# Scatters of a batch as 16 pairs behind named matmul groups, and fills of the last batch as plain DMAs on SP's queue

## The chip, the cores and the metric

The kernel runs on one core of a Trainium2 chip. The metric is the device time of one execution in microseconds (us). The kernel before takes 2137.58 us, the median of three runs (2136.33 to 2138.60).

## The reference

A transformer block over 16 sequences of 512 tokens with 256 features: a layer norm, causal attention with 16 heads of 16 dimensions and rotary positions, a mixture of 32 experts of which each token uses 4, and a shared feed-forward part.

```python
xn = _layernorm(x)
x = x + attention(xn, Wq, Wk, Wv, Wo) + ffn(xn, ...)

# the mixture, for every token n of the 16 * 512
scores = softmax(flat @ router_w.T + router_bias)
topk_scores, topk_idx = top_k(scores, 4)
topk_scores = topk_scores / topk_scores.sum(-1)
h = silu(flat @ gate_w[e].T) * (flat @ up_w[e].T)      # each expert e
out = sum over the 4 chosen e of topk_scores * (h @ down_w[e].T)
out = out + silu(flat @ sgate_w.T) * (flat @ sup_w.T) @ sdown_w.T
```

## The kernel before

There are three phases, with a barrier of all engines between them.

**Phase A** (phase_a) goes over the 16 batches (sequences). For a batch it computes attention, the shared feed-forward part and the routing, and writes each normalised token to four places in DRAM, one for each expert chosen. The tensor values has a region of 8192 rows for each of the 32 experts, and an expert's tokens lie there from the region's start; table has an entry (token number, weight) for each row. **Phase BC** (phase_bc) takes the experts' rows in 288 blocks of 128, applies the expert, and scatters the results into y_dram. **Phase D** (phase_d) sums a token's four results and the rest, and stores them.

A block of phase BC is read whole, so the rows behind an expert's last token, up to the block's end, must hold something harmless. The last batch of phase A therefore also writes 128 rows of zeros behind each expert's last token. This is the step fill.

Phase A is one list of steps, ORDER, which every engine walks through in the same order and in which it takes the steps that it has a handler for. The matrix multiplications of a step run on TensorE (PE), and the same names stand for the copies and exponentials on ScalarE (ACT), the reductions on VectorE (DVE) and the sums on GpSimd (POOL). The list mixes two batches: attention and feed-forward steps of batch b, and projection and routing steps of batch b+1 (NEXT_STEPS). An engine does its steps strictly in turn, so an instruction that waits holds all behind it on that engine. Batch 0 has its own copy of the list, batches 1 to 14 run in a loop, and the last batch has a shorter list (last_steps) without the steps of a next batch, with the fills and with the loads of the experts' weights (load_gu, load_d, on ACT's DMA queue).

The steps that matter here:

- qk(t), t from 0 to 3, projects and rotates 128 tokens of the next batch. PE multiplies (L911), DVE applies the tables (L706, L709), POOL sums (L472, rqk). Then the values are split in three bf16 parts in turns: ACT part0 (L542), POOL the rest (L474), ACT part1 (L547), POOL the last part (L476). PE transposes the parts in partsT(t) (L923), and ACT copies them (L564).
- s1(g, u) and s2(g, u) are score products of head group g: s1 feeds a maximum on DVE (L745), s2 an exponential on ACT (L607). The two share two PSUM units, so that an s1 or s2 may start on PE when the DVE or ACT instruction that reads the unit is through.
- negT(g) passes the maxima through PE and ACT (L595) and a small store on SP's DMA queue (L403) to the operand of s2(g, ...).
- scat(t), t from 0 to 3, sends four of the 16 scatter pairs of a batch. A pair is one indirect DMA for table (L487) and one for values (L489), of 128 rows each. They are issued by POOL, which makes their descriptors in software. scat(0) and scat(1) stand near the start of a batch, scat(2) and scat(3) behind the last qk, partsT and route.
- fill sends 32 indirect DMAs (L495) from POOL behind scat(3) of the last batch. Rows past an expert's region are given a number out of bounds and skipped.
- At the start, SP clears table with one DMA (L414), behind the 24 stack DMAs (L384), and then loads xres (L396) and the tokens of batch 1 (L390), which DVE's lnA (L670) waits for. All of these stand on one queue.

Phase A ends when SP has seen the last store of sum_dram (L409) land, POOL has seen the fills and scatters land, and ACT the weights.

## Time and profile before

| what | value |
|---|---|
| time, median of three runs | 2137.58 us |
| time, lowest and highest | 2136.33, 2138.60 us |
| span of the profiled execution | 2641.3 us |
| PE busy | 1935.0 us, 73% |
| DVE busy | 1290.2 us, 49% |
| ACT busy | 929.5 us, 35% |
| POOL busy | 1063.8 us, 40% |
| granted TensorE clock, mean | 0.847 of full speed |
| phase A, BC, D (in the profiled execution) | to 1945 us, 561 us, 135 us |

The profile is of one execution, recorded by the hardware. Its span goes from the first to the last instruction; no other time of this execution is given. The span is 503.7 us above the median of the runs without a profile, and this difference has to be kept in mind wherever a duration or a wait is read from the trace. Busy times are sums over an engine's instructions; a matrix multiplication's end is modelled. In a row of the trace the first number is the start in us from the span's start, the second the duration, and what stands in square brackets is how long the engine sat idle before it and what ended the idleness.

### The profile page before, as it was taken

The page shows a single profiled execution, that of the slowest core. Times are in us where ns is not written, and L with a number is a line of the kernel's source. Part 1 is how long each engine was busy: PE and PEld are TensorE (multiplying, and loading weights), DVE is VectorE, ACT ScalarE, POOL GpSimd, SP SyncE. Part 2 cuts the span into 40 slices and gives each one's busy share as a digit, 9 for nine tenths or more (in the row PEclk, how much of TensorE's full clock was granted, in tenths as well). Part 3 has the DMA queues.
Part 4 walks back from the last instruction along what each step waited for, and adds up shares of the span by engine and source line. Part 5 has one row for each costly group of instructions (what it writes and reads, how often), then busy time and mean ns, then how long its engine had stood idle before and what let it go on. Part 6 is the DMA issues. An engine that isn't in the chain of part 4 may idle for free. (4 is left out here: it accounts for less than half of the span.)

```text
span 2641.3 us, 43971 instructions
## 1 busy us (share of the span) xinstructions
PE 1935.0 (73%) x11495; PEld 1234.2 (47%) x11496; DVE 1290.2 (49%) x3379; ACT 929.5 (35%) x1953; POOL 1063.8 (40%) x1056
## 2 busy tenths in 40 slices
PE   5677778787767878777887877874479898998900
PEld 2344444444434444444544444442257777777700
DVE  4445345364534536453453535442235555555567
...
GB/s 107 63 97 21 93 40 64 64 40 96 19 94 40 64 64 40 96 22 90 47 57 88 17 100 30 78 59 76 132 158 159 153 150 146 155 144 152 112 304 331
DMA packets 242512, 255.07 MB, mean 97 GB/s; under 512 B 74357, under 2 KB 216190, under 8 KB 242304
## 3 DMA queue, kind: packets, MB, share of 16 engines
...
q14 instruction: 60, 0.49, 0.1%
...
## 5 line engine op out<-in xcount | busy, mean ns | idle before, releaser
L745 DVE TENSOR_REDUCE neg<-ps_u 128x2 f32<-128x768 f32 (+3 forms) x384 | 392.4, 1043 | 380.7 <-PE ps_u L952 237.2
L487 POOL DMA_INDIRECT table<-entry,slot x256 | 248.0, 969 | 536.2 <-ACT xs L585 435.4
L982 PE MATMUL ps_u<-we_d 99*128 99x512 bf16 (+3 forms) x1024 | 246.1, 353 | 250.1 <-DMA we_d<-neg_t 121.6
L607 ACT ACTIVATE probs<-ps_u 128x1024 f32<-128x1024 f32 x320 | 323.1, 1027 | 286.6 <-PE ps_u L993 189.2
L1244 POOL DMA_INDIRECT y_dram<-yb,ent x288 | 283.0, 983 | 278.8 <-issue 164.9
L489 POOL DMA_INDIRECT values<-xs,slot x256 | 252.3, 986 | 83.4 <-issue 83.4
L933 PE MATMUL ps_g<-we_gu 128*128 128x512 f32 x512 | 257.7, 634 | 38.1 <-DVE hid L728 32.1
L949 PE MATMUL ps_u<-we_d 96*128 96x128 bf16 (+3 forms) x1024 | 232.2, 312 | 72.4 <-ACT probs L607 26.6
L982 PEld LDWEIGHTS ps_u<-we_d 99*128 99x128 bf16 x1024 | 96.5, 107 | 397.5 <-issue 221.4
L911 PE MATMUL ps_g<-we_gu 128*128 128x512 f32 (+1 forms) x512 | 199.7, 514 | 2.4 <-ACT we_gu L564 2.4
L472 POOL TENSOR_TENSOR rqk<-we_gu 128x512 f32<-128x512 f32 x64 | 81.3, 1270 | 266.2 <-DVE we_gu L709 263.3
L767 DVE RECIPROCAL rden<-ps_g 128x16 f32<-128x16 f32 x64 | 16.3, 255 | 348.8 <-issue 250.2
L1281 PE MATMUL ps_av<-we_gu,x_t 128*128 x576 | 157.9, 399 | 36.5 <-DVE x_t L1369 34.5
L1012 PE MATMUL ps_av<-probs,v_pad 128*32 128x512 f32 (+3 forms) x2048 | 165.9, 447 | 23.8 <-issue 22.6
L949 PEld LDWEIGHTS ps_u<-we_d 96*128 96x128 bf16 x1024 | 94.1, 100 | 190.5 <-issue 59.8
L1295 PE MATMUL ps_u<-we_d,h_t 128*128 x576 | 177.6, 391 | 0.0
L952 PE MATMUL ps_u<-mask_qk,identb 128*128 128x128 bf16 (+2 forms) x704 | 177.2, 252 | 0.0
L993 PE MATMUL ps_u<-mask_kq,identb 128*128 128x256 bf16 (+1 forms) x640 | 132.6, 291 | 52.1 <-issue 52.1
L933 PEld LDWEIGHTS ps_g<-we_gu 128*128 128x128 f32 x512 | 97.2, 200 | 132.1 <-issue 80.5
L1281 PE MATMUL ps_g<-we_gu,x_t 128*128 x576 | 155.4, 394 | 4.1 <-issue 4.1
L1369 DVE COPY x_t<-ps_g 128x256 f32<-128x256 f32 x288 | 120.6, 419 | 67.9 <-issue 44.8
L616 ACT ACTIVATE av<-ps_av 128x512 f32<-128x512 f32 x64 | 37.8, 591 | 299.6 <-remote 212.1
...
## 6 DMA issues: line engine op xcount, KB each, us to landing
we_d<-we_gu SPq DMA_DIRECT2D x384, 128.0 KB, 5.9
xg<-values SPq DMA_DIRECT2D x288, 128.0 KB
ys<-y_dram SPq DMA_DIRECT2D x64, 512.0 KB, 5.4
we_gu<-x SPq DMA_DIRECT2D x16, 512.0 KB
xres<-x SPq DMA_DIRECT2D x16, 512.0 KB
sum_dram<-osum SPq DMA_DIRECT2D x16, 512.0 KB, 3.2
we_gu<-wgu_e ACTq DMA_DIRECT2D x16, 512.0 KB
...
```

The source lines that it names most:

```text
L487: pool.indirect_dma_start(table[:, :], bass.IndirectOffsetOnAxis(ap=slot[:, k:k + 1], axis=0), entry[:, k, :], None).then_inc(scattered, 16)
L489: pool.indirect_dma_start(values[:, :], bass.IndirectOffsetOnAxis(ap=slot[:, k:k + 1], axis=0), xs[:, k // TOPK, :], None).then_inc(scatte ...
L607: nc.scalar.activation(probs[g % 2][:, u, :], ps_u[env[1][step][0]][:, :, :].rearrange("p a n -> p (a n)"), ACT.Exp, scale=SCALE).then_inc ...
L745: nc.vector.tensor_reduce(neg[:, g % 2, i, h0:h0 + nh], src, AX.X, ALU.max, negate=True).then_inc(S["row_max"], 1)
L911: ins = nc.tensor.matmul(ps[:, 0:n], xn_t[:, c, t * P:(t + 1) * P], w_qkvr[:, c, lo:lo + n], start=(c == 0), stop=(c == KC - 1))
L933: ins = nc.tensor.matmul(ps[:, :], w_gu[:, c, lo:lo + P], xn_t[:, c, :], start=(c == 0), stop=(c == KC - 1))
L949: nc.tensor.matmul(ps[:, a, k * n:(k + 1) * n], q_st[0:KROWS, h, i * P:(i + 1) * P], k_st[0:KROWS, h, 0:n], start=(k == 0), stop=False, sk ...
L952: ins = nc.tensor.matmul(dst, identb[:], mask_qk[:].rearrange("p (o n) -> p o n", o=1).broadcast_to([P, per_bank, P]), start=False, stop=T ...
L982: nc.tensor.matmul(ps[:, a, lo:lo + n], k_st[0:MROWS, h, kt * P:(kt + 1) * P], q_st[0:MROWS, h, kt * P:SEQ], start=(lo == 0), stop=False, ...
L1244: pool.indirect_dma_start(y_dram[:, :], bass.IndirectOffsetOnAxis(ap=ent[k][:, 0:1], axis=0), yb[k][:, :], None, bounds_check=TOKENS * TOP ...
L1281: ins = nc.tensor.matmul(ps_gu[s][:, 0:2 * HE], x_t[s][:, c * P:(c + 1) * P], w_gu[:, bass.ds(e, 1), c, :], start=(c == 0), stop=(c == KC ...
L1295: nc.tensor.matmul(ps_y[s][:, 0:D], h_t[s][:], w_d[:, bass.ds(e, 1), :], start=True, stop=True).then_inc(y_ps, 1)
```

## The change

The four steps scat(t) of four pairs each become 16 steps scat(k) of one pair each, spread over the whole list. Before a pair POOL waits until PE has done the group of matmuls that the table SCAT_AFTER names; the step stands right behind that group in ORDER. The old waits for xs and slot stay, at the first pair. All other steps keep their order, and PE and ACT have the same instructions as before.

The fills leave POOL. In the last batch the step fill(k) stands behind negT(k), k from 0 to 3, in SP's list. SP loads 8 row numbers into registers and issues 8 plain DMAs of 128 rows of zeros. So that no row is skipped, the last 128 rows of every region are zeroed at the start, in one DMA of 4.19 MB on SP's queue ahead of the DMA that clears table, and an expert whose tokens reach into these rows gets its fill placed in the region of the expert with the fewest tokens. DVE computes the row numbers with 10 small instructions in place of 5. Two setup steps go (row_p, and wider buffers).

```diff
@@ -73,22 +73,29 @@
 
 ORDER = [
     ("rankC",), ("gate", 0), ("placeV",), ("s1", 0, 0), ("gth", 0), ("up", 0), ("s1", 0, 1), ("copy",), ("s1", 0, 2),
-    ("gate", 1), ("s1", 0, 3), ("s1", 0, 4), ("gth", 1), ("scat", 0), ("up", 1), ("lnA",), ("gate", 2), ("s1", 0, 5),
-    ("negsplit", 0), ("gth", 2), ("scat", 1), ("s1", 1, 0), ("up", 2), ("s1", 1, 1), ("negT", 0), ("gate", 3),
-    ("lnB",), ("lnC",), ("gth", 3), ("up", 3), ("s2", 0, 0), ("s2", 0, 1), ("s2", 0, 2), ("s1", 1, 2), ("xT", 0),
-    ("xT", 1), ("xT", 2), ("s1", 1, 3), ("s1", 1, 4), ("qk", 0), ("s2", 0, 3), ("vr", 0), ("xT", 3), ("vr", 1),
-    ("part0", 0), ("s1", 1, 5), ("negsplit", 1), ("s2", 0, 4), ("qk", 1), ("part1", 0), ("negT", 1), ("s1", 2, 0),
-    ("s1", 2, 1), ("part0", 1), ("av", 0, 0), ("av", 0, 1), ("s1", 2, 2), ("s2", 1, 0), ("av", 0, 2), ("av", 0, 3),
-    ("s1", 2, 3), ("partsT", 0), ("s1", 2, 4), ("s1", 2, 5), ("part1", 1), ("avT", 0), ("qk", 2), ("s2", 1, 1),
-    ("s2", 1, 2), ("negsplit", 2), ("partsT", 1), ("s2", 1, 3), ("part0", 2), ("qk", 3), ("s2", 1, 4), ("negT", 2),
-    ("part1", 2), ("vr", 2), ("s1", 3, 0), ("s1", 3, 1), ("part0", 3), ("av", 1, 0), ("av", 1, 1), ("av", 1, 2),
-    ("av", 1, 3), ("s1", 3, 2), ("s2", 2, 0), ("partsT", 2), ("s1", 3, 3), ("part1", 3), ("s1", 3, 4), ("s2", 2, 1),
-    ("avT", 1), ("s2", 2, 2), ("s2", 2, 3), ("vr", 3), ("s1", 3, 5), ("negsplit", 3), ("route",), ("partsT", 3),
-    ("scat", 2), ("s2", 2, 4), ("negT", 3), ("av", 2, 0), ("av", 2, 1), ("av", 2, 2), ("av", 2, 3), ("s2", 3, 0),
-    ("scat", 3), ("s2", 3, 1), ("avT", 2), ("stack", 0), ("s2", 3, 2), ("s2", 3, 3), ("rank",), ("s2", 3, 4),
+    ("gate", 1), ("s1", 0, 3), ("scat", 0), ("s1", 0, 4), ("gth", 1), ("up", 1), ("scat", 1), ("lnA",), ("gate", 2),
+    ("s1", 0, 5), ("scat", 2), ("negsplit", 0), ("gth", 2), ("s1", 1, 0), ("up", 2), ("scat", 3), ("s1", 1, 1),
+    ("negT", 0), ("gate", 3), ("lnB",), ("lnC",), ("gth", 3), ("up", 3), ("scat", 4), ("s2", 0, 0), ("s2", 0, 1),
...
+SCAT_AFTER = [("s1", 0, 3), ("up", 1), ("s1", 0, 5), ("up", 2), ("up", 3), ("s1", 1, 2), ("s2", 0, 4), ("s2", 1, 0),
+              ("s1", 2, 5), ("s2", 1, 3), ("s1", 3, 1), ("s2", 2, 0), ("s2", 2, 3), ("s2", 2, 4), ("s2", 3, 0),
+              ("s2", 3, 3)]
...
@@ -103,8 +110,8 @@
         s.append(step)
         if step == ("rankC",):
             s.append(("fill_rows",))
-        if step == ("scat", NT - 1):
-            s.append(("fill",))
+        if step[0] == "negT":
+            s.append(("fill", step[1]))
         if step[0] == "s2" and step[1:] != (0, 0) and piece < GU_PIECES:
             s.append(("load_gu", piece))
             piece += 1
@@ -410,13 +420,28 @@
 
             def loaded(b, step, env):
                 if step[1] == 1:
+                    sp.wait_ge(consts, N_EARLY)
+                    sp.dma_start(values.rearrange("(e r) d -> r e d", e=E)[REGION - P:REGION, :, :],
+                                 zeros[:].rearrange("p (o d) -> p o d", o=1).broadcast_to([P, E, D])).then_inc(ends_set, 16)
                     sp.wait_ge(inited, 1)
                     sp.dma_start(table.rearrange("(p r) c -> p (r c)", p=P),
                                  probs[0][:, :, :].rearrange("p u n -> p (u n)")[:, 0:2 * TABLE // P].bitcast(I32)
                                  ).then_inc(table_set, 16)
 
-            run(sp, {"loaded": loaded, "stack": stack_rows, "gate": gate, "negT": neg_store, "oproj": store})
+            def fill(b, step, env):
+
+                k, n = step[1], E // NG
+                if k == 0:
+                    sp.wait_ge(fill_ready, 1)
+                    sp.wait_ge(ends_set, 16)
+                _, rows = nc.values_load_multi_w_load_instructions(
+                    fill_row[0:1, k * n:(k + 1) * n], engines=(mybir.EngineType.SP,), min_val=0, max_val=E * REGION - P)
+                for row in rows:
+                    sp.dma_start(values[bass.ds(row, P), :], zeros[:, :]).then_inc(filled, 16)
+
+            run(sp, {"loaded": loaded, "stack": stack_rows, "gate": gate, "negT": neg_store, "oproj": store, "fill": fill})
             sp.wait_ge(sum_out, 16 * BATCH)
+            sp.wait_ge(filled, 16 * E)
...
@@ -479,22 +502,22 @@
                     chain.closed()
 
             def scatter(b, step, env):
-                t = step[1]
-                pool.wait_ge(xs_ready, NT * b + NT)
-                pool.wait_ge(slots, b + 1)
+                k = step[1]
+                after = SCAT_AFTER[k]
+                if after[0] == "s1":
+                    pool.wait_ge(pe["s1"], NG * NU1 * b + NU1 * after[1] + after[2] + 1)
+                elif after[0] == "s2":
+                    pool.wait_ge(pe["s2"], NG * NU2 * b + NU2 * after[1] + after[2] + 1)
+                else:
+                    pool.wait_ge(pe["up"], NM * b + after[1] + 1)
+                if k == 0:
+                    pool.wait_ge(xs_ready, NT * b + NT)
+                    pool.wait_ge(slots, b + 1)
                 hold(pool, passed_pool)
-                for k in range(TOPK * t, TOPK * (t + 1)):
-                    pool.indirect_dma_start(table[:, :], bass.IndirectOffsetOnAxis(ap=slot[:, k:k + 1], axis=0),
-                                            entry[:, k, :], None).then_inc(scattered, 16)
-                    pool.indirect_dma_start(values[:, :], bass.IndirectOffsetOnAxis(ap=slot[:, k:k + 1], axis=0),
-                                            xs[:, k // TOPK, :], None).then_inc(scattered, 16)
-
-            def fill(b, step, env):
-                pool.wait_ge(fill_ready, 1)
-                for e in range(E):
-                    pool.indirect_dma_start(values[:, :], bass.IndirectOffsetOnAxis(ap=fill_row[:, e:e + 1], axis=0),
-                                            zeros[:, :], None, bounds_check=E * REGION - 1, oob_is_err=False
-                                            ).then_inc(filled, 16)
+                pool.indirect_dma_start(table[:, :], bass.IndirectOffsetOnAxis(ap=slot[:, k:k + 1], axis=0),
+                                        entry[:, k, :], None).then_inc(scattered, 16)
+                pool.indirect_dma_start(values[:, :], bass.IndirectOffsetOnAxis(ap=slot[:, k:k + 1], axis=0),
+                                        xs[:, k // TOPK, :], None).then_inc(scattered, 16)
 
             def loaded(b, step, env):
...
@@ -850,17 +872,23 @@
 
             def fill_rows(b, step, env):
 
-                nc.vector.tensor_scalar(fill_f[:, 0, :], counts[:], row_p[:, 0:1], None, ALU.add).then_inc(fill_chain, 1)
-                dve.wait_ge(fill_chain, 1)
-                nc.vector.tensor_scalar(fill_f[:, 1, :], fill_f[:, 0, :], float(REGION), float(SKIP), ALU.is_ge,
-                                        ALU.mult).then_inc(fill_chain, 1)
-                dve.wait_ge(fill_chain, 2)
-                nc.vector.tensor_tensor(fill_f[:, 0, :], fill_f[:, 0, :], fill_f[:, 1, :], ALU.add).then_inc(fill_chain, 1)
-                dve.wait_ge(fill_chain, 3)
-                nc.vector.scalar_tensor_tensor(out=fill_f[:, 1, :], in0=iota_e[:], scalar=float(REGION),
-                                               in1=fill_f[:, 0, :], op0=ALU.mult, op1=ALU.add).then_inc(fill_chain, 1)
-                dve.wait_ge(fill_chain, 4)
-                nc.vector.tensor_copy(fill_row[:], fill_f[:, 1, :]).then_inc(fill_ready, 1)
+                made = [0]
+
+                def link(ins):
+                    made[0] += 1
+                    ins.then_inc(fill_chain, 1)
+                    dve.wait_ge(fill_chain, made[0])
+                link(nc.vector.tensor_scalar(fill_f[:, 0, :], counts[0:1, :], -1.0, None, ALU.mult))
+                link(nc.vector.max(least_v[:], fill_f[:, 0, :]))
+                link(nc.vector.max_index(least_i[:], least_v[:], fill_f[:, 0, :]))
+                link(nc.vector.tensor_copy(spare[:], least_i[:, 0:1]))
+                link(nc.vector.tensor_scalar(spare[:], spare[:], float(REGION), float(REGION - P), ALU.mult, ALU.add))
+                link(nc.vector.tensor_tensor(fill_f[:, 0, :], counts[0:1, :], region[0:1, :], ALU.add))
+                link(nc.vector.tensor_scalar(fill_f[:, 1, :], fill_f[:, 0, :], -1.0, spare[:, 0:1], ALU.mult, ALU.add))
+                link(nc.vector.scalar_tensor_tensor(out=fill_f[:, 1, :], in0=counts[0:1, :], scalar=float(REGION - P),
+                                                    in1=fill_f[:, 1, :], op0=ALU.is_gt, op1=ALU.mult))
+                link(nc.vector.tensor_tensor(fill_f[:, 0, :], fill_f[:, 0, :], fill_f[:, 1, :], ALU.add))
+                nc.vector.tensor_copy(fill_row[:], fill_f[:, 0, :]).then_inc(fill_ready, 1)
```

The instructions of POOL in a batch of the loop, around the second and third qk, before:

```order
L472 TENSOR_TENSOR rqk<-we_gu 128x512
L474 TENSOR_TENSOR we_gu<-rqk,we_gu 128x512
L476 TENSOR_TENSOR we_gu<-we_gu 128x512
L468 REGISTER_ALU
L472 TENSOR_TENSOR rqk<-we_gu 128x512
L474 TENSOR_TENSOR we_gu<-rqk,we_gu 128x512
L476 TENSOR_TENSOR we_gu<-we_gu 128x512
```

And the same place now, qk(1), the pairs 7 and 8, and qk(2) (the lines are those of the changed kernel):

```order
L495 TENSOR_TENSOR rqk<-we_gu 128x512
L497 TENSOR_TENSOR we_gu<-rqk,we_gu 128x512
L499 TENSOR_TENSOR we_gu<-we_gu 128x512
L510 REGISTER_ALU
L517 DMA table<-entry,slot 262272x2
L519 DMA values<-xs,slot 262144x256
L508 REGISTER_ALU
L517 DMA table<-entry,slot 262272x2
L519 DMA values<-xs,slot 262144x256
L491 REGISTER_ALU
L495 TENSOR_TENSOR rqk<-we_gu 128x512
L497 TENSOR_TENSOR we_gu<-rqk,we_gu 128x512
```

Between the steps of qk on POOL there stood nothing before. Now there is one pair between qk(0) and qk(1), two between qk(1) and qk(2), and one between qk(2) and qk(3).

SP's queue at the start of the program, between the stack DMAs and the first load for batch 1, before:

```order
L384 DMA we_d<-we_gu 16x8x512 x24
L414 DMA table<-probs 128x4098
L396 DMA xres<-x 128x4x256
L390 DMA we_gu<-x 128x4x256
```

And now:

```order
L394 DMA we_d<-we_gu 16x8x512 x24
L424 DMA values<-zeros 128x32x256
L427 DMA table<-probs 128x4098
L406 DMA xres<-x 128x4x256
L400 DMA we_gu<-x 128x4x256
```

The zeros stand ahead of three transfers that other engines wait for.

## Rows read from the trace of the kernel before

**Rows 1.** Span of the profiled execution and mean granted clock.

```profile
core 0: 2641.3 us, clock 0.847
```

**Rows 2.** Busy time by engine in stretches; the first row names the columns.

```profile
core 0: us, PE busy (x) PEld busy (x) DVE busy (x) ACT busy (x) POOL busy (x), PEclk, DMA share, GB/s
1067.00:1084.00 17.00, 3.52 (x12) 1.08 (x10) 0.95 (x4) 0.81 (x2) 10.02 (x11) 0.57 0.82 140
1084.00:1120.00 36.00, 35.33 (x188) 22.33 (x186) 18.39 (x48) 10.97 (x18) 7.82 (x9) 0.92 0.54 98
1120.00:1135.60 15.60, 3.97 (x8) 1.35 (x8) 4.52 (x16) 1.06 (x2) 7.66 (x8) 0.84 0.13 43
1135.60:1182.40 46.80, 44.49 (x344) 25.94 (x348) 31.34 (x62) 29.95 (x47) 20.10 (x18) 0.94 0.02 6
1806.00:1881.00 75.00, 6.66 (x25) 2.54 (x23) 2.60 (x3) 4.25 (x5) 52.13 (x54) 0.53 0.25 90
1945.00:2506.00 561.00, 503.12 (x2599) 411.46 (x2599) 302.49 (x1165) 239.41 (x864) 282.25 (x291) 0.94 0.49 144
2506.00:2641.00 135.00, 0.00 (x0) 0.00 (x0) 96.33 (x192) 0.00 (x0) 1.41 (x2) 0.50 0.87 311
```

**Rows 3.** Timeline of PE in a steady batch: start, us, instruction.

```profile
1072.19 0.48 PE L982 MATMUL ps_u<-we_d 99*128 99x384 bf16 x1 [1.53 <-issue]
1076.80 0.27 PE L993 MATMUL ps_u<-mask_kq,identb 128*128 128x128 bf16 x1 [2.11 <-issue]
...
1135.61 1.03 PE L982 MATMUL ps_u<-we_d 99*128 99x512 bf16 x3 [8.69 <-DMA we_d<-neg_t]
...
1159.45 0.60 PE L982 MATMUL ps_u<-we_d 99*128 99x512 bf16 x3
```

**Rows 4.** Timeline of POOL over qk(1) to qk(3) of that batch.

```profile
1151.34 1.28 POOL L472 TENSOR_TENSOR rqk<-we_gu 128x512 f32<-128x512 f32 x1 [0.24 <-DVE we_gu L709]
...
1158.35 1.15 POOL L476 TENSOR_TENSOR we_gu<-we_gu 128x512 bf16<-128x512 f32 x1 [3.84 <-ACT we_gu L547]
1161.31 1.26 POOL L472 TENSOR_TENSOR rqk<-we_gu 128x512 f32<-128x512 f32 x1 [1.80 <-DVE we_gu L709]
1165.10 1.15 POOL L474 TENSOR_TENSOR we_gu<-rqk,we_gu 128x512 f32<-128x512 f32 x1 [2.52 <-ACT we_gu L542]
...
1168.39 1.27 POOL L472 TENSOR_TENSOR rqk<-we_gu 128x512 f32<-128x512 f32 x1 [0.17 <-POOL we_gu L476]
...
1175.10 0.98 POOL L487 DMA_INDIRECT table<-entry,slot  x1 [0.15 <-issue]
1176.39 0.97 POOL L489 DMA_INDIRECT values<-xs,slot  x1 [0.30 <-issue]
```

**Rows 5.** Timeline of ACT in the same stretch.

```profile
1152.65 0.63 ACT L542 ACTIVATE we_gu<-rqk 128x512 bf16<-128x512 f32 x1 [1.70 <-POOL rqk L472]
...
1164.36 0.66 ACT L542 ACTIVATE we_gu<-rqk 128x512 bf16<-128x512 f32 x1
...
1169.70 0.63 ACT L542 ACTIVATE we_gu<-rqk 128x512 bf16<-128x512 f32 x1 [2.42 <-POOL rqk L472]
...
1170.71 1.01 ACT L607 ACTIVATE probs<-ps_u 128x1024 f32<-128x1024 f32 x1
```

**Rows 6.** Timeline of PE behind it: s1(3, 4), whose unit the exponential frees.

```profile
1171.78 0.39 PE L949 MATMUL ps_u<-we_d 96*128 96x512 bf16 x1
```

**Rows 7.** The instructions of line L487: duration in ns, least, median, most.

```profile
L487 POOL DMA_INDIRECT table<-entry,slot x256: 962/967/1141, 74.2 to 1830.8; - x128
```

**Rows 8.** Timeline of SP, then DVE, at the start of the program.

```profile
55.47 0.62 SPq L414 DMA_DIRECT2D table<-probs  x1
...
75.72 1.41 DVE L670 BATCH_NORM_STATS2 stats<-we_gu 128x6 f32<-128x256 f32 x4 [9.67 <-DMA we_gu<-x]
```

**Rows 9.** DMA issues of the last store: KB each, us from issue to landing.

```profile
sum_dram<-osum SPq DMA_DIRECT2D x16, 512.0 KB, 3.2
```

**Rows 10.** Timeline of POOL and SP at the end of phase A.

```profile
1792.57 0.97 POOL L487 DMA_INDIRECT table<-entry,slot  x1 [29.38 <-ACT xs L585]
...
1833.31 1.00 POOL L495 DMA_INDIRECT values<-zeros,fill_row  x1 [0.30 <-issue]
...
1873.30 0.98 POOL L495 DMA_INDIRECT values<-zeros,fill_row  x1 [0.30 <-issue]
...
1945.13 0.37 POOL L1232 IOTA blk_i<- 32x288 f32 x1 [70.85 <-POOLq L193]
...
1941.71 0.42 SPq L409 DMA_DIRECT2D sum_dram<-osum  x1
```

19 lines of the change are left out of this document (11 added, 8 removed), and 9 rows, old and new, of the table ORDER.

## The prediction

> **What bounds the kernel now.** I began with the span [rows 1]: 2641.3 us, 503.7 us above the median of the timed runs. A difference of 24% decides what the rest may be read for, so the first question is where those 503.7 us lie.
>
> The stretches of a steady batch of phase A answer it [rows 2]. From 1067 to 1182.4 us, one period of 115.4 us, PE has two bad stretches: 17.0 us with 3.5 us of work, and 15.6 us with 4.0 us. In the other 82.8 us it is busy for 79.8. In the bad stretches DVE and ACT stand too (0.8 to 4.5 us busy), and POOL alone works: it is issuing its bursts of indirect DMAs. PE then starts one small matmul every 2 us or so and "waits for nothing that the profile shows" (the gaps marked issue) [rows 3]. In the last batch the burst is longest, pairs and then fills, and the standstill is 75 us with 6.7 us of PE work. Together the idle part is 15 x (32.6 - 7.5) + (75 - 6.7) = 377 + 68 = 445 us. After a stretch PE also runs at the lower clock for a while: the same three matmuls take 1.03 us at 1135.61 and 0.60 us at 1159.45 [rows 3], and the granted clock is 0.57 in the first stretch and 0.94 in the last [rows 2]. The 59 us that are missing to 503.7 would be 3.9 us a batch, which fits.
>
> Could the difference lie elsewhere? Phase BC has PE busy for 503 of 561 us, and phase D has the DMA engines at 0.87 of 135 us [rows 2]. If all their slack went, that gives 58 + 18 = 76 us. So at least some 430 of the 504 us must be the standstills. I conclude that the timed runs hardly have them: they belong to the profiled execution. A timed batch is then 115.4 - 25.1 - 3.9 = 86.4 us and bound by PE, with the chain through POOL and ACT close behind. That is the reading on which all hangs. Whatever the change does to them is worth little in the metric, and it has to be priced on the rest.
>
> **Steady batches: four of the 16 pairs enter a chain.** A pair costs POOL 2 x 1.27 = 2.55 us (start to start, 1175.10 to 1176.39, twice) [rows 4]. In the kernel before all 16 stand where POOL has nothing else to do. Now one stands between qk(0) and qk(1), two between qk(1) and qk(2), one between qk(2) and qk(3). The matmul groups that they wait for are through by then, so it is the 2.55 us that count, not the new wait. POOL's gaps there are 0.24, 1.80 and 0.17 us [rows 4]. Step by step:
> - qk(1) starts 2.5 us later than 1151.34. Its last sum (1158.35) had waited 3.84 us for ACT [rows 4], which absorbs most of it: it ends about 0.9 us late.
> - The pairs 7 and 8 take 5.1 us and find a gap of 1.8: qk(2) starts 0.9 + 5.1 - 1.8 = 4.2 us late. Its second sum (1165.10) had waited 2.52 us for ACT [rows 4], whose part0(2) began at 1164.36 [rows 5]. ACT would now be waiting for POOL there, and about 1.5 us are absorbed: qk(2) ends 2.7 us late.
> - Pair 9 adds 2.55 and finds 0.17: qk(3) starts 5.1 us late.
>
> ACT waits for exactly this instruction: part0(3) at 1169.70, idle 2.42 us before it. Behind it in ACT's order stands the exponential at 1170.71, which ends at 1171.72 [rows 5], and PE begins s1(3, 4), which needs that unit, at 1171.78 [rows 6]. There is no slack, so PE is 5.1 us late, and since it is the bound, the batch is. 15 batches prepare a next one: 15 x 5.1 = 76.5 us. Bounds for a batch: nothing, if the timed run has slack that these rows don't show, and 10.2 - 2.2 = 8.0 us if nothing is absorbed. A gain at this place would need leftover standstills, and is a rival below. I take 5.1. The pairs 10 to 15 follow behind qk(3), 6 x 2.55 = 15.3 us, and are wanted only at the next batch's rankC, half a batch later: nothing.
>
> One rule speaks against spreading the pairs. The longest of the 256 table scatters took 1141 ns against a median of 967 [rows 7], though many ran beside DVE's work. The Trainium skill (SBUF — State Buffer, section "SBUF: two separate sides") says that DVE, in a mode that takes the shared port pair, locks GpSimd out of writing descriptors, and gives 3100 ns for a DMA of 620 ns; by that, eight DMAs in the qk stretch would cost an estimated 20 us a batch. The trace shows nothing of that size, and I keep it as a rival only.
>
> **Start of the program: 4.19 MB of zeros.** They go ahead of the clearing of table and of x for batch 1 on one queue. DVE waited 9.67 us for x, until 75.72 [rows 8], with its later steps and PE behind it, so a delay of this queue counts whole. At the 311 GB/s of phase D [rows 2] they take 13.5 us; at the pace of the 512 KB store, 3.2 us each [rows 9], 25.6 us; nothing, if they overlap with the stack DMAs. I take 13.5, since the queue is in order and phase D is the nearest row with many transfers in flight.
>
> **Last batch.** POOL's work from the first pair (1792.57) to the last fill's end (1874.3) is 81.7 us, with a landing of about 3.2 us 85 [rows 9, 10]. The other path, to the store at 1941.71 and the barrier at 1945.13 [rows 10], is 152.6 us, less the 75 of the standstill, plus 6.7 to 10 for its work, less up to 5 for the clock: 79 to 88 us. So POOL's fills are a bound of at most 6 us, and taking them off gains 0 to 6: I take 3. SP now issues 8 fills behind each store of negT. At 0.62 us [rows 8] that is 5 us, and with the registers' loads perhaps 8; the next store is due about 20 us later (four in 83 us), and 1.05 MB take 3.4 us at the rate above. I count nothing; without that cover it is 3 x 5 = 15 us. DVE has five instructions more ahead of s1(0, 0), at up to 0.35 us each (a quarter of 1.41) [rows 8], 0 to 1.8: I take 1.
>
> **Sum.** 2137.6 + 76.5 + 13.5 - 3 + 1 = 2225.6, rounded 2225 us, 4.1% slower. In the profiled execution the sum stands against 2641.3: that loses most of the 503.7 us and gains the same 88, so I expect a span of 2220 to 2330. It would be a large gain in the profile beside a loss in the metric.
>
> **Rivals.**
> - *The chain has slack in timed runs.* The batches cost 0 to 1 us, and the start and the end decide: 2137.6 + 11.5 + 0 to 8 = about 2150 us. For it: the timed runs never showed me their order. Against it: the 0.06 us between ACT's exponential and PE [rows 5, 6]. If the zeros are hidden too, no change.
> - *The standstills are partly real.* The slack elsewhere allows up to 76 us of them in the timed runs, 5 us a batch, and a part of the last batch's, say 10. Pairs with pauses remove them. If half of the chain's delay stays, 2137.6 - 85 + 38 + 11.5 = about 2100 us, faster. It decides from the point where a timed batch holds more standstill than 5.1 us. For it: at 1.95 us a DMA phase BC (561 us for 288) shows no such stop, so pauses do help. Against it: PE's busy share outside.
> - *Nothing is absorbed.* 8.0 us a batch and 25.6 us at the start: 2137.6 + 120 + 26 = about 2283 us.
> - *DVE holds up the scatters in the chain.* As a mechanism here: each of the 8 DMAs of the four pairs waits for one DVE instruction of up to 1 us, 8 us more a batch, and 2225 + 120 = 2345 us. Rows 7 speak against it. That is the skill's rule, priced by this kernel's own instructions.
>
> **How the numbers follow.** The forecast has 0.60, with its own range 2185 to 2255. The slack has 0.14, the real standstills 0.16, nothing absorbed 0.06, DVE's hold 0.04. A difference of 0.2% (4 us) is about what this measurement can tell from none. Faster: nearly all of the second rival, 0.15. Same: a part of the first and the edge of the second, 0.05. Slower: 0.80. The range from 2125 to 2260 leaves out 0.1 below and 0.1 above.
>
> **What would show it.** In the changed kernel's profile: no stretch in which PE, DVE and ACT stand while POOL issues, or short ones only behind qk(3); a span of 2220 to 2330; pairs of 2.55 us between L472's groups on POOL; the wait of ACT's part0(3) grown from 2.4 us to 5 or more, with PE idle before s1(3, 4) as long; a period of about 91.5 us; DVE's wait for x grown from 9.67 us to about 23. The prediction is wrong if the time goes down, which would mean that timed runs have standstills, or if the period is 87 us, which would mean that the chain absorbs the pairs.

## The result, and the profile after

The changed kernel takes 2178.84 us (median of 4 runs, 2173.63 to 2185.87) beside 2136.95 us for the kernel before (2134.82 to 2138.6). The ratio is 1.0203, with an interval of 1.0181 to 1.0225: 42 us slower, where 88 were forecast.

The kernels were timed in sessions, each with the kernel before beside the others, and there are two kinds: in some sessions the kernel before takes about 2137 us, in the others about 2626 us, and all its times in one session agree within 0.5%. The comparison above is of the first kind. The first recording of the kernel before (2641.3 us) looks like the second, so its rows and the profile after can't be compared stage by stage. A new recording of the kernel before in the first kind is used for that (before_again, below).

Span and mean clock of the changed kernel, which answer to [rows 1]:

```profile
core 0: 2184.0 us, clock 0.935
```

Two stretches of it, one batch and phase BC. The columns are those of [rows 2].

```profile
849.70:940.00 90.30, 82.00 (x558) 48.85 (x556) 54.41 (x126) 42.63 (x68) 45.53 (x45) 0.98 0.42 76
1542.60:2048.00 505.40, 484.55 (x2599) 398.91 (x2599) 302.66 (x1165) 240.13 (x864) 281.82 (x290) 0.98 0.54 159
```

There are no standstills here: a batch has PE busy for 82.0 of 90.3 us at a clock of 0.98, where [rows 2] had 3.52 of 17.0 us at 0.57 in a bad stretch. Phase BC has the same 2599 matmuls in 505 us where [rows 2] had 561.

POOL in the changed kernel, from qk(1) to behind qk(3), which answers to [rows 4]:

```profile
849.79 1.28 POOL L495 TENSOR_TENSOR rqk<-we_gu 128x512 f32<-128x512 f32 x1
...
856.51 0.98 POOL L517 DMA_INDIRECT table<-entry,slot  x1 [0.15 <-issue]
857.80 0.98 POOL L519 DMA_INDIRECT values<-xs,slot  x1 [0.30 <-DVE we_gu L731]
859.08 0.97 POOL L517 DMA_INDIRECT table<-entry,slot  x1 [0.30 <-issue]
860.35 0.97 POOL L519 DMA_INDIRECT values<-xs,slot  x1 [0.30 <-issue]
861.34 1.28 POOL L495 TENSOR_TENSOR rqk<-we_gu 128x512 f32<-128x512 f32 x1
...
866.65 0.99 POOL L517 DMA_INDIRECT table<-entry,slot  x1 [0.15 <-POOL we_gu L499]
867.94 0.97 POOL L519 DMA_INDIRECT values<-xs,slot  x1 [0.30 <-issue]
868.93 1.27 POOL L495 TENSOR_TENSOR rqk<-we_gu 128x512 f32<-128x512 f32 x1
```

Two pairs (856.51 to 861.3) stand between qk(1) and qk(2), one (866.65 to 868.9) between qk(2) and qk(3). The next sum starts with no idle time of POOL before it: POOL is what the chain waits for. No DMA of these rows is longer than 0.99 us, though DVE works beside them, and of all 256 table scatters of this run the median takes 967 ns and the longest 1282. The rival of DVE's hold, which asked for up to 1 us more on each of the 8 DMAs, is out.

ACT and then PE behind qk(3), which answer to [rows 5, 6]:

```profile
870.24 0.63 ACT L564 ACTIVATE we_gu<-rqk 128x512 bf16<-128x512 f32 x1 [4.70 <-POOL rqk L495]
...
871.25 1.02 ACT L629 ACTIVATE probs<-ps_u 128x1024 f32<-128x1024 f32 x1
```

```profile
872.32 0.61 PE L977 MATMUL ps_u<-we_d 96*128 96x512 bf16 x1 [2.67 <-ACT probs L629]
```

ACT's wait for POOL has grown from 2.42 us to 4.70, and PE now stands 2.67 us for ACT's exponential.

The start of the program, SP and then DVE, which answer to [rows 8]:

```profile
56.37 0.63 SPq L424 DMA_DIRECT2D values<-zeros  x1
57.04 26.79 SPq L427 DMA_DIRECT2D table<-probs  x1
83.87 0.45 SPq L406 DMA_DIRECT2D xres<-x  x1
```

```profile
104.23 1.41 DVE L692 BATCH_NORM_STATS2 stats<-we_gu 128x6 f32<-128x256 f32 x4 [37.35 <-DMA we_gu<-x]
```

The issue behind the zeros takes SP 26.79 us, and DVE starts batch 1 at 104.23 where it was 75.72.

The end of phase A, SP and then POOL, which answer to [rows 10]:

```profile
1471.32 5.81 SPq L440 DMA_DIRECT2D values<-zeros  x8
...
1498.47 4.03 SPq L440 DMA_DIRECT2D values<-zeros  x8
```

```profile
1523.42 0.97 POOL L519 DMA_INDIRECT values<-xs,slot  x1 [0.30 <-issue]
1542.56 0.37 POOL L1260 IOTA blk_i<- 32x288 f32 x1 [18.18 <-POOLq L200]
```

Eight fills cost SP 4.0 to 5.8 us (the first and the third of the four groups are shown), and POOL has issued its last scatter 18 us ahead of its first instruction behind the barrier.

### The profile page after: what moved, and what is told of

Same layout as the page of the kernel before. It is cut to its first block and busy times, and to the rows that moved or that the text cites. A ratio compares the mean times of both kernels' runs of the same rounds, so it can differ in the third digit from the quotient of the medians.

```text
span 2184.0 us, 44481 instructions
## 1 busy us (share of the span) xinstructions
PE 1819.7 (83%) x11495; PEld 1186.8 (54%) x11496; DVE 1276.7 (58%) x3385; ACT 925.1 (42%) x1953; POOL 1031.5 (47%) x1023
## 5 line engine op out<-in xcount | busy, mean ns | idle before, releaser
L629 ACT ACTIVATE probs<-ps_u 128x1024 f32<-128x1024 f32 x320 | 318.1, 1023 | 149.0 <-PE ps_u L1021 147.7
L961 PE MATMUL ps_g<-we_gu 128*128 128x512 f32 x512 | 243.7, 609 | 3.0 <-DVE gth L742 2.9
L1010 PE MATMUL ps_u<-we_d 99*128 99x512 bf16 (+3 forms) x1024 | 204.9, 314 | 27.4 <-DMA we_d<-neg_t 10.9
L1040 PE MATMUL ps_av<-probs,v_pad 128*32 128x512 f32 (+3 forms) x2048 | 156.1, 440 | 1.6 <-ACT probs L629 1.4
L1309 PE MATMUL ps_g<-we_gu,x_t 128*128 x576 | 150.4, 384 | 4.3 <-issue 4.3
L1309 PE MATMUL ps_av<-we_gu,x_t 128*128 x576 | 149.9, 383 | 1.5 <-issue 1.5
L1404 DVE TENSOR_SCALAR wh<-ent 128x1 f32<-128x1 f32 x288 | 44.3, 154 | 174.4 <-ACT tnh L1219 131.4
L599 ACT ACTIVATE we_gu<-ps_g 128x512 f32<-128x512 f32 x64 | 38.2, 597 | 221.0 <-PE ps_g L961 221.0
L1233 ACT ACTIVATE yb<-ps_u 128x256 f32<-128x256 f32 x288 | 110.6, 384 | 31.1 <-PE ps_u L1323 4.8
L1070 PE MATMUL ps_u<-w_d,hid 128*128 128x256 f32 x512 | 121.7, 386 | 1.3
```

Of the source, the lines that this page charges most:

```text
L629: nc.scalar.activation(probs[g % 2][:, u, :], ps_u[env[1][step][0]][:, :, :].rearrange("p a n -> p (a n)"), ACT.Exp, scale=SCALE).then_inc ...
L961: ins = nc.tensor.matmul(ps[:, :], w_gu[:, c, lo:lo + P], xn_t[:, c, :], start=(c == 0), stop=(c == KC - 1))
L1010: nc.tensor.matmul(ps[:, a, lo:lo + n], k_st[0:MROWS, h, kt * P:(kt + 1) * P], q_st[0:MROWS, h, kt * P:SEQ], start=(lo == 0), stop=False, ...
L1309: ins = nc.tensor.matmul(ps_gu[s][:, 0:2 * HE], x_t[s][:, c * P:(c + 1) * P], w_gu[:, bass.ds(e, 1), c, :], start=(c == 0), stop=(c == KC ...
```

## The experiments

### The kernel before, recorded again

No edit.

> The kernel before, unchanged, profiled once more. If the standstills belong to the recording of POOL's bursts of DMAs, the span is again about 2640 us while the time is 2137 us, and the batches have a period of about 115 us. If they were an accident of that one recording (phase BC, whose code the change doesn't touch, also took 561 us there and 494 us in the changed kernel's profile), the span is near 2137 us and the period is 88 to 89 us.

Measured: 2134.03 us, in a session in which nine other runs of it gave a median of 2136.16. Its span is 2132.2 us, so the first recording's 2641.3 was not a cost that every recording adds. A whole burst of 16 scatter DMAs here, and a whole one of the first recording (columns of [rows 2]):

```profile
638.30:658.70 20.40, 18.36 (x163) 12.02 (x161) 8.20 (x34) 11.11 (x16) 15.83 (x16) 1.00 0.72 132
```

```profile
830.10:850.50 20.40, 8.36 (x71) 4.17 (x69) 5.88 (x24) 4.83 (x8) 15.80 (x16) 0.76 0.58 105
```

Over the whole burst PE is busy for 18.36 of 20.4 us, and in the first recording for 8.36; the 3.52 of 17.0 us of [rows 2] are the worst part of such a burst. The code is the same and POOL's DMAs take as long. So the standstills are no property of the code alone.

This recording gives the base for the sum. Phase A's chain and phase BC can be read off first and last starts (in the form "first to last start"). The views by tile, of POOL's first sum of each qk (64 of them) and of DVE's copies in phase BC (288), in the kernel before:

```profile
L472 POOL TENSOR_TENSOR rqk<-we_gu x64: 1259/1272/1282, 16.0 to 1319.0; 128x512 f32<-128x512 f32 x64
```

```profile
L1369 DVE COPY x_t<-ps_g x288: 415/417/426, 1463.9 to 1991.1; 128x256 f32<-128x256 f32 x144
```

and in the changed kernel:

```profile
L495 POOL TENSOR_TENSOR rqk<-we_gu x64: 1259/1274/1286, 16.4 to 1414.8; 128x512 f32<-128x512 f32 x64
```

```profile
L1397 DVE COPY x_t<-ps_g x288: 415/418/426, 1554.8 to 2042.7; 128x256 f32<-128x256 f32 x144
```

The table, in us, is worked out from these rows and those of the other kernels in sessions of the first kind. "Phase BC" is from the first to the last copy of x_t, and the span is the four columns and the 15.5 to 16.4 us ahead of the first qk:

| kernel | first to last qk | last qk to phase BC | phase BC | rest | span |
|---|---|---|---|---|---|
| before_again | 1303.0 | 144.9 | 527.2 | 141.1 | 2132.2 |
| after | 1398.4 | 140.0 | 487.9 | 141.3 | 2184.0 |
| pairs_only | 1373.8 | 165.7 | 529.1 | 142.3 | 2227.1 |
| fills_only | 1330.3 | 138.2 | 487.0 | 140.7 | 2112.4 |
| fills_late | 1322.5 | 138.4 | 487.1 | 140.2 | 2104.2 |
| chain_free_4 | 1367.7 | 144.0 | 487.1 | 140.6 | 2155.7 |
| dve_pad_2 | 1306.5 | 146.1 | 487.6 | 140.8 | 2096.5 |

The changed kernel's 51.8 us more of span than before_again are +95.4, -4.9, -39.3 and +0.6, the last with the 0.4 us ahead of the first qk. (Its recorded run is 7 us above its median and that of before_again 2 below; the medians differ by 42.)

### The pairs alone, the fills alone

```diff
 pairs_only: ORDER, SCAT_AFTER and scat of the changed kernel, and
+        if step == ("scat", NT - 1):        # NT is 16 pairs here
+            s.append(("fill",))             # POOL's 32 indirect fills, as before
 fills_only: the kernel before with the changed kernel's fills, zeros and fill_rows
```

> Only the scatters are spread in 16 pairs; the fills stay on POOL and no zeros are written at the start. Theory: the pairs in the chain cost 1.4 to 2 us in each of 15 batches (what the changed kernel leaves when 28.5 us are taken off for the start), and POOL's fills now follow pair 15, which is issued behind s2(3, 3), so 41 us of fills end some 25 us after the main path: 2137 + 25 + 25 = about 2187 us. Rival (the prediction's chain of 5.1 us a batch): 2137 + 76 + 25 = about 2238 us. Rival (pairs cost nothing): about 2162 us. The profile's period of a batch, 90.3 us in the changed kernel, must stay; the end of phase A is to be read apart.

> The scatters stand as before, four steps of four pairs; the fills go over SP's queue, with the zeros at the start. Theory: the start costs 28.5 us (DVE's wait for x ended at 104.2 in place of 75.7 us) and the end gains 0 to 10: 2155 to 2166 us. Rival (the prediction's 13.5 us for the start): 2137 + 13.5 - 3 = about 2148 us.

Measured: pairs_only 2224.26 us, ratio 1.041 (1.0388 to 1.0432); fills_only 2113.75 us, ratio 0.9892 (0.9877 to 0.9907). Neither agrees with what was expected. pairs_only comes near the rival at 2238 us, the prediction's own chain, and not the theory's 2187. fills_only lies 41 us under the lower end of its theory and 34 under its rival, because of phase BC (below).

The pairs lengthen the stretch of the qk steps by 70.8 us, 4.7 a batch. The fills add 27.3 there, nearly all of it the delay of batch 1 (DVE starts it at 102.07, in before_again at 75.97). Together that is 98.1, and the changed kernel has 95.4. So in this stretch the two add up: the longer batches belong to the pairs and the late start to the fills.

Two columns say more. With the pairs alone the end of phase A becomes 20.8 us longer: the pairs are issued later in the last batch, and POOL's 32 fills stand behind them. With both edits this is gone. And phase BC, which neither edit touches, takes 40.2 us less with the fills alone and 1.9 more with the pairs alone.

### The zeros later, and earlier

```diff
 fills_late, against fills_only
-                    (the DMA of zeros ahead of the clearing of table)
+                    if isinstance(b, int) and b == 0:      # behind the loads of xres and x for batch 1
+                        sp.wait_ge(consts, N_EARLY)
+                        sp.dma_start(values...[REGION - P:REGION, :, :], zeros...).then_inc(ends_set, 16)
 zeros_early, against fills_only, and after_early, against the changed kernel
             sp.dma_start(w_o[:, :, :], ...).then_inc(weights, 16)
+            sp.wait_ge(consts, N_EARLY)
+            sp.dma_start(values...[REGION - P:REGION, :, :], zeros...).then_inc(ends_set, 16)
```

> As fills_only, but the DMA of the zeros stands behind the loads of xres and x for batch 1 on SP's queue. Theory: the whole cost of the start goes, and what is left is the end: 2137 less 0 to 10 us, 2127 to 2137 us. Rival: the zeros also delay what comes behind them (the stores of negT of batch 0), and half of the 28.5 us stays: about 2148 us.

> The version with only the last batch's fills changed, with the 4.19 MB transfer of zeros issued on SP right behind the load of w_o at the start, where the DMA engines carry little between 14 and 40 us. Theory A (the start of batch 1 is late because the zeros stand ahead of x in the DMA engines, 102.1 against 76.0 us in the run of the fills alone): DVE's first instruction on batch 1's x starts near 76 us, batch 15's osum ends some 20 to 25 us earlier than the fills alone (1466.5), and the time is about 2113.75 - 25 = 2089 us (2080 to 2100). Theory B (the late store of batch 0's negT in the version with zeros behind x shows that 28 us of DMA work delay whatever they meet): the zeros now delay the loads of the first weights and x of batch 0, the time stays at 2105 to 2115.

> The changed kernel with its 4.19 MB of zeros issued right behind the load of w_o instead of behind batch 0's stack_rows. Theory A (the zeros hold up x of batch 1): the start becomes some 26 us shorter on any chip, that is about 2153 us where the kernel before takes 2137 and about 2328 us where it takes 2625. Theory B (28 us of DMA work cost the same wherever they stand): no change, 2179 or 2354 us.

Measured: fills_late 2104.91 us, ratio 0.9851 (0.9836 to 0.9866). Its x for batch 1 is in time (75.61 us), but a store of negT's operand then stands behind the zeros, and PE waits for it:

```profile
102.07 1.01 PE L997 MATMUL ps_u<-we_d 99*128 99x512 bf16 x3 [15.13 <-DMA we_d<-neg_t]
```

Only 9 of some 27 us were saved, as the rival said; that the time is still 22 us under the theory's 2127 is phase BC again. The other two ran in sessions of the second kind: zeros_early 2571.23 us beside 2628.01 for the kernel before (ratio 0.9784, 0.9757 to 0.981), and again (zeros_early_2) 2566.43 beside 2627.79 (0.9776, 0.9756 to 0.9796); after_early 2322.97 us beside 2627.79 (0.8855, 0.8835 to 0.8875). The changed kernel itself took 2353.54 in another session of that kind (beside 2624.74), so the earlier zeros gain 31 us, to within the few us by which such sessions differ. SP and DVE in after_early:

```profile
54.93 0.61 SPq L427 DMA_DIRECT2D table<-probs  x1
```

```profile
75.56 1.41 DVE L692 BATCH_NORM_STATS2 stats<-we_gu 128x6 f32<-128x256 f32 x4 [10.11 <-DMA we_gu<-x]
```

The clearing of table is issued in 0.61 us and DVE starts at 75.56 as in the kernel before. It was the place of the transfer, theory A. In the first kind of session the early zeros weren't timed; an estimate is fills_only less the 26 to 27 us of its late start, about 2087.

> The fills alone with early zeros, for its time where the kernel before takes about 2137 us: theory A 2080 to 2100 us (2113.75 for the fills alone, less some 25 us at the start), theory B 2105 to 2115 us. Where the kernel before takes about 2625 us it takes 2571 us again.

### Six more instructions on DVE

```diff
                 dve.wait_ge(fill_chain, 4)
+                for k in range(6):
+                    nc.vector.tensor_scalar(fill_f[:, 1, :], fill_f[:, 1, :], 0.0, None, ALU.add).then_inc(fill_chain, 1)
+                    dve.wait_ge(fill_chain, 5 + k)
```

> The kernel before with six more small instructions on DVE in the step that works out the fill rows (fill_f plus zero, each waiting for the one before; the values are not changed) and nothing else. Theory A (the gain of 40 us in the last two phases comes from where DVE's loop of phase BC lies among the blocks in which its instructions are fetched: each of 8 rounds of the loop loses 3.3 to 4.6 us in the kernel before and in the pairs alone, whose DVE programs have the same length, and none in the fills alone, whose DVE program has 5 instructions more): phase BC (first to last copy of x on DVE) goes from 527 to about 487 us, the time to 2137 - 40 + 1 = 2098 us. Theory B (the shorter program of POOL, the longer of SP, or the zeros' transfer makes the gain): phase BC stays at 527 us and the time at 2136 to 2139 us.

> The kernel before with six more small instructions on DVE, for its time where the kernel before takes about 2137 us. Theory A (the length of DVE's program ahead of the loop of phase BC decides on 40 us): phase BC 487 us, 2098 us. Theory B: 527 us, 2137 us. Where the kernel before takes about 2625 us: 2592 us again.

Measured: 2095.40 us beside 2136.23, ratio 0.9805 (0.9786 to 0.9825), and in the second kind of session 2592.66 beside 2628.01 (0.9866, 0.9849 to 0.9882). Six instructions that do nothing make the kernel before 41 us faster. Phase BC takes 487.6 us, like that of every kernel with the changed fill_rows. This is what goes: DVE and then PE in before_again, at one of seven such places in the loop of phase BC:

```profile
1552.38 0.42 DVE L1369 COPY x_t<-ps_g 128x256 f32<-128x256 f32 x1 [5.77 <-issue]
```

```profile
1552.95 1.53 PE L1281 MATMUL ps_av<-we_gu,x_t 128*128 x4 [4.09 <-DVE x_t L1369]
```

The view of the tile x_t, first in before_again (what DVE waited for, and who waited for it), then in dve_pad_2:

```profile
its engine sat idle before it (us, times) until:
  issue: 89.5, 38
...
who waited for it (us, times):
...
  PE ps_av L1281: 32.0, 7
```

```profile
  issue: 18.1, 46
```

The loop has eight turns of 32 blocks. In before_again DVE stops seven times, some 60 us apart (1552.38, 1612.51, 1672.92 and so on), for 5.77 to 6.65 us each, and it stops ahead of the copies of blocks 49, 81, 113 and so on to 241, which are the first copies of turns two to eight. PE's seven waits behind them, 32.0 us together, are gone in dve_pad_2 and in the changed kernel, and DVE's idle time in which nothing held it falls from 89.5 to 18.1 us (18.3 in the changed kernel). The rest of the 39.6 us of phase BC wasn't followed further. The page of the profile counts 3379 instructions on DVE in before_again and in pairs_only, and 3385 in the five kernels whose phase BC takes 487 to 488 us. Six is also what the changed fill_rows adds: it has five operations more, and its max_index is two instructions in the trace. Nothing in phase BC differs, and the extra ones stand ahead of it. dve_pad_2 has the programs of POOL and SP of the kernel before and no DMA of zeros at the start. So what counts is where DVE's loop lies in its program. The Trainium skill (Runtime: NRT & Kernel Launch, section "Instruction fetch mechanics") says that instructions are fetched in blocks of 256 and that a taken branch whose target isn't among the blocks held forces a fetch and a stall. The rows agree with that, a stall of 5.77 us and more with no releaser at each of the seven branches back; that it is the fetch is not shown by them.

### No pair between qk(0) and qk(3)

```diff
 ORDER of the changed kernel, with pairs 0 to 6 ahead of ("qk", 0) and 7 to 15 behind ("qk", 3)
+SCAT_AFTER = [("s1", 0, 3), ("up", 1), ("s1", 0, 5), ("up", 2), ("up", 2), ("up", 3), ("s1", 1, 2), ("s1", 3, 1),
+              ("s1", 3, 1), ("s2", 2, 0), ("s2", 2, 0), ("s2", 2, 3), ("s2", 2, 4), ("s2", 3, 0), ("s2", 3, 0),
+              ("s2", 3, 3)]
```

> The changed kernel with the same 16 pairs and waits, but none of them between qk(0) and qk(3) on POOL: pairs 0 to 6 stand ahead of qk(0), pairs 7 to 15 behind qk(3). Theory A (a batch is 4.5 us longer because four pairs of 2.55 us stand in POOL's qk chain, on which part0 and s1 wait): the period goes from 90.28 back to about 85.8 us and the time to 2179 - 15 x 4.5 = 2111 us (2100 to 2125). Theory B (the pairs cost time by their number or by their traffic, wherever they stand): the period stays near 90 us and the time at 2170 to 2185 us.

> No pair between qk(0) and qk(3), once more for its time where the kernel before takes about 2137 us. Theory A (four pairs in the chain make a batch 4.5 us longer there): period 85.8 us, 2100 to 2125 us. Theory B (number, not place): 2170 to 2185 us. Where the kernel before takes about 2625 us: 2415 us again.

Measured in the first kind of session (chain_free_4): 2157.08 us, ratio to the kernel before 1.0096 (1.0077 to 1.0116), between the two theories. The stretch of the qk steps is 1367.7 us, 30.7 less than in the changed kernel: 2.0 a batch, of 4.5. POOL's first sums of one batch's qk(0) and qk(3), in the kernel before (before_again), the changed kernel and chain_free_4, the last with the first pair ahead of them:

```profile
694.09 1.26 POOL L472 TENSOR_TENSOR rqk<-we_gu 128x512 f32<-128x512 f32 x1
...
716.75 1.27 POOL L472 TENSOR_TENSOR rqk<-we_gu 128x512 f32<-128x512 f32 x1 [0.17 <-POOL we_gu L476]
```

```profile
752.24 1.26 POOL L495 TENSOR_TENSOR rqk<-we_gu 128x512 f32<-128x512 f32 x1 [1.68 <-DVE we_gu L731]
...
779.18 1.27 POOL L495 TENSOR_TENSOR rqk<-we_gu 128x512 f32<-128x512 f32 x1
```

```profile
718.76 0.97 POOL L515 DMA_INDIRECT table<-entry,slot  x1 [16.67 <-PE ps_u L978]
...
739.22 1.28 POOL L493 TENSOR_TENSOR rqk<-we_gu 128x512 f32<-128x512 f32 x1
...
761.73 1.27 POOL L493 TENSOR_TENSOR rqk<-we_gu 128x512 f32<-128x512 f32 x1 [0.17 <-POOL we_gu L497]
```

From qk(0) to qk(3) it is 22.66, 26.94 and 22.51 us. Of the other batches behind the first, nearly all agree within 0.2 us (two in the changed kernel have 29.6). The four pairs make the chain 4.28 us longer, and without them it is short again. What PE waits for ahead of s1 between 700 and 1060 us, some four batches (us in total, times, longest us), in the same three kernels:

```profile
PE ps_u L949 <- DVE neg L745: 4.3, 9, 2.2
...
PE ps_u L949 <- ACT probs L607: 0.3, 2, 0.2
```

```profile
PE ps_u L977 <- ACT probs L629: 18.6, 8, 5.4
```

```profile
PE ps_u L975 <- DVE neg L765: 9.8, 8, 2.3
...
PE ps_u L975 <- ACT probs L627: 0.6, 4, 0.2
```

In the changed kernel PE waits 18.6 us for ACT's exponential, 4.6 a batch where the batch is 4.5 longer. Without pairs in the chain this wait is gone again (0.6), so the path of the prediction, from POOL over ACT to s1, is shown. But PE then waits longer for DVE's maximum, 9.8 us against 4.3. Seven pairs ahead of qk(0) wait 16.67 us for a named group of PE and then run straight up to 739.22, where qk(0) starts with no idle time before it. The test took away one delay and brought in another. Which of them makes up the 2.5 us a batch that are left wasn't separated, and theory A's 2111 us was missed by 46.

In sessions of the second kind the same kernel took 2419.37, 2415.29 and 2411.61 us (chain_free, chain_free_2, chain_free_3), beside 2628.01, 2624.74 and 2627.79 for the kernel before.

> The changed kernel with no pair between qk(0) and qk(3) again, for its time on a chip with about 2137 us for the kernel before. There, theory A (four pairs of 2.55 us in POOL's qk chain make the batch 4.5 us longer): period 85.8 us, time 2100 to 2125 us. Theory B (the pairs cost by number, not by place): 2170 to 2185 us. On a chip with 2628 us it takes 2419 us again, and theory S expects the changed kernel beside it to be faster than that, since this one's bursts are longer (10, 2, 2, 12 and 6).

> No pair between qk(0) and qk(3), for its time where the kernel before takes about 2137 us. Theory A (four pairs in the chain make a batch 4.5 us longer there): period 85.8 us, 2100 to 2125 us. Theory B (number, not place): 2170 to 2185 us. Where the kernel before takes about 2625 us it takes 2417 us again.

### The changed kernel where the standstills are

No edit.

> The changed kernel once more, beside the kernel before on the same chip. The last four kernels ran on a chip on which the kernel before takes 2628 us, as in its first recording (2641.3), where the earlier ones ran beside 2137 us. Theory S (the standstills belong to the chip, and come where POOL issues its indirect DMAs in one long burst: from the seventh DMA of a burst on PE, DVE and ACT stop until it ends): on a chip with about 2630 us for the kernel before, the changed kernel, whose bursts are 2, 4, 8 and 12 DMAs where the kernel before has 16 and 16, loses less, 2230 to 2400 us, so it is faster there; on a chip with 2137 us it takes 2179 us again. Theory R (the standstills cost the changed kernel what they cost the kernel before, some 490 us): 2650 to 2700 us on the first kind of chip.

Measured: 2353.54 us beside 2624.74 for the kernel before, ratio 0.898 (0.8959 to 0.9). The change that costs 2.0% in one kind of session gains 10.2% in the other. Theory R falls. Theory S's range holds, but not its "belong to the chip" (below, on the hardware), and the changed kernel's bursts in a steady batch are of at most 8 DMAs here, where it had named 12 (as many as in the first kind of session). Two of the bursts in one batch, of 6 and 8 DMAs (columns of [rows 2]):

```profile
753.00:760.30 7.30, 5.79 (x40) 3.83 (x38) 3.40 (x13) 3.74 (x7) 5.78 (x6) 0.82 0.10 36
...
800.30:810.20 9.90, 7.29 (x34) 3.39 (x33) 8.82 (x26) 2.21 (x3) 7.74 (x8) 1.00 0.11 41
```

PE is busy for 5.79 of 7.3 and 7.29 of 9.9 us there, where it had 8.36 of 20.4 in the burst of 16 above. The changed kernel is still 175 us slower here than in the first kind of session. Of the 167 us between the two recordings 135 lie in the stretch of the qk steps, 9 a batch, and 31 in phase BC, whose scatters don't stand in such bursts. So this kind of session costs something outside the long bursts too.

### The waits and the place of the pairs, apart

```diff
 no_wait, against the changed kernel
+                if k > 0:
+                    pass
-                if after[0] == "s1":
+                elif after[0] == "s1":
 chain_six: ("scat", 10) and ("scat", 11) stand behind ("scat", 9), ahead of ("qk", 3), and wait for ("s2", 1, 3) as it does
```

> The changed kernel without the waits of pairs 1 to 15 for a named matmul group; the pairs stand where they stood on POOL. On a chip with 2137 us for the kernel before: theory O (the cost is that the pairs occupy POOL inside the qk chain): 2170 to 2190 us, period 90.3 us. Theory W (the cost is that POOL waits for PE's groups ahead of the pairs and comes late to qk): period below 88 us, time below 2145 us. On a chip with 2628 us: theory S expects it slower than the changed kernel, by 20 us or more, if the waits break bursts up; the same if the order alone does.

> The changed kernel with pairs 10 and 11 moved forward, from behind qk(3) to right behind pair 9, ahead of qk(3): six of the pairs are in the qk chain where four were. Theory A (each pair in the chain delays its end by its own time once slack is used up): the period grows by 2 x 2.55 = 5.1 us to about 95.4 us and the time by 15 x 5.1 = 76 us to about 2255 us. Theory B (the number or the traffic of the pairs costs, not the place): no change, 2170 to 2190 us. Theory C (PE's other work covers a part of it): 2200 to 2240 us.

> The changed kernel with pairs 10 and 11 in the qk chain too, again for its time on a chip with about 2137 us for the kernel before. Theory A: period 95.4 us, time about 2255 us (each pair in the chain 2.55 us). Theory C (other work of PE covers a part): 2200 to 2240 us. Theory B (place does not matter): 2170 to 2190 us. On a chip with 2628 us: 2365 us again.

> The changed kernel without the waits of pairs 1 to 15 for a named matmul group, once more for its time where the kernel before takes about 2137 us. Theory O (the pairs occupy POOL in the qk chain, from the start of qk(0) to that of qk(3) 26.9 us against 22.7 in the kernel before): period 90.3 us, 2170 to 2190 us. Theory W (it is the waits): below 88 us and below 2145 us. Where the kernel before takes about 2625 us: 2508 us again.

All four runs fell in sessions of the second kind. no_wait: 2508.20 us beside 2624.74 (0.9562, 0.9534 to 0.9591), and 2517.86 beside 2624.59 (0.9582, 0.9563 to 0.9601). chain_six: 2365.31 beside 2628.01 (0.8996, 0.8982 to 0.901), and 2361.14 beside 2624.74 (0.8995, 0.8974 to 0.9016). Ordered by the longest bursts in a steady batch (DMAs that POOL issues with less than 0.8 us between them):

| kernel | bursts in a batch | time, us |
|---|---|---|
| after_again | at most 8 | 2353.5 |
| chain_six_2 | at most 8 | 2361.1 |
| chain_free_2 | 10, 12, 6 | 2415.3 |
| no_wait | 12, 12 | 2508.2 |
| before | 16, 16 | 2624.7 |

Without the waits for named groups the bursts are longer and the time is 155 us more, as theory S expected ("20 us or more"). That the length of the bursts makes the difference is argued from this order, not tested by itself. Two whole bursts of 12 in no_wait:

```profile
705.80:720.90 15.10, 8.74 (x68) 4.39 (x66) 5.83 (x24) 5.75 (x8) 11.68 (x12) 0.84 0.12 45
595.40:610.40 15.00, 5.78 (x40) 3.84 (x38) 6.39 (x26) 4.27 (x7) 11.60 (x12) 0.73 0.12 44
```

PE has 8.74 us of work in 15.1, and in the other 5.78 in 15.0.

Does the wait or the place make the chain longer? POOL's first sums of qk(0) and qk(3) in no_wait:

```profile
779.78 1.27 POOL L495 TENSOR_TENSOR rqk<-we_gu 128x512 f32<-128x512 f32 x1 [12.38 <-DVE we_gu L733]
...
806.72 1.27 POOL L495 TENSOR_TENSOR rqk<-we_gu 128x512 f32<-128x512 f32 x1
```

Again 26.94 us, as with the waits. It is the place, as theory O says. Whether no_wait takes 2170 to 2190 us in the first kind of session was not seen. Nor was chain_six seen there, so the price of a fifth and a sixth pair is open. In the second kind two more pairs cost 8 us in all, not theory A's 76, although the chain does get longer by their 5.1 us: in chain_six_2 qk(0) and qk(3) start at 724.57 and 756.64, 32.07 us apart, and in after_again at 719.35 and 746.28, 26.93 apart. PE's wait for the exponential ahead of s1 grows with it, from 16.2 to 36.6 us between 700 and 1100 us. What gives the time back wasn't found; one thing that changes is that the burst right behind qk(3) is of 4 DMAs in place of 8. So a longer chain doesn't cost its length everywhere.

## Why the prediction was wrong

The sign was right, the size was twice what was measured: 88 us forecast, 42 found. Two terms of the sum failed, DVE's added instructions (+1, measured -39.3 by way of phase BC) and the zeros at the start (13.5, measured 28.3), and the reading of the standstills on which the pricing stood failed as a statement. By its own steps:

- **The standstills "belong to the profiled execution".** The working from span to 86.4 us a batch was good for the session in which the change was timed: a batch of before_again takes 85.7 (694.09 to 779.78), and no burst stops PE there (18.36 of 20.4 us busy). As a statement it fell. The standstills come with the session, and where they are, all timed runs have them: 2624.6 to 2628.0 us in four sessions. Each of these runs left a span and a clock as well (2626.63 us has a span of 2624.8), and the changed kernel's recorded run is one of its four timed ones, so no run here shows what one without any recording takes. That recording has a part in the standstills is not ruled out. The forecast "a large gain in the profile beside a loss in the metric" mixed two kinds of session; each is consistent in itself. The rival "the standstills are partly real" was nearer in that pairs with pauses go with fewer of them (after_again), but not for these timed runs.
- **Steady batches, 15 x 5.1 = 76.5 us.** Measured 95.4 less 28.3 for the start, 67.1 us or 4.5 a batch, and 70.8 or 4.7 with the pairs alone. The steps can be followed in the rows: counted from qk(0), POOL's qk(1), qk(2) and qk(3) start 2.2, 3.8 and 4.3 us later than in before_again, where 2.5, 4.2 and 5.1 were forecast, ACT's wait is 4.70 where 5 or more was expected, and PE waits 4.6 us a batch for the exponential. The mechanism was right, and the forecast 14% above the measured term: more was absorbed in qk(1) and qk(2).
- **Start, 13.5 us.** DVE starts batch 1 at 104.23 where before_again has 75.97: 28.3 us. The step that failed here is the pace: 311 GB/s of phase D was chosen, and 4.19 MB in 28 us are an estimated 150 GB/s. The other bound, 25.6 us from the rows of the 512 KB store, was the near one and even that was passed.
- **Last batch, -3 us.** Measured -4.9, and -6.7 with the fills alone. What was missed is that the pairs alone would have made this end 20.8 us longer, because they push POOL's fills back; moving the fills to SP takes that off. Eight fills on SP took 4.0 to 5.8 us, about the 5 that were counted.
- **DVE's five instructions, +1 us.** This is the step that failed most. They were priced where they stand, 0 to 1.8 us (the trace has six). They also move the loop of phase BC within DVE's program, and that gave 39.3 us back. That a stage which the change doesn't touch could change was not among the rivals.

The terms, forecast and measured: 76.5 and 67.1, 13.5 and 28.3, -3 and -4.9, 1 and -38.7 (phase BC and the rest). The sum is 88 and 51.8 on the recorded runs, 42 on the medians. Without the 39.3 us of phase BC the kernel would be at about 2218 us, and the forecast of 2225 would have looked exact while its second term was off by half.

The range of 2125 to 2260 held the time, and the forecast's own of 2185 to 2255 missed it by 6 us. Of the signs that were named, the period is 90.3 us in the batch shown (91.5 forecast) the wait of part0(3) 4.70 us (5 or more), the wait for x 37.35 us (about 23) and the span 2184.0 (2220 to 2330). The rivals: the chain has no slack in the first kind of session, DVE does not hold the scatters, and what is absorbed is small.

Versions that beat both kernels: where the kernel before takes 2137 us, dve_pad_2 (2095.4), fills_late (2104.9) and fills_only (2113.8); where it takes 2626, after_early (2323.0).
